# Adding a residual on VectorE out of PSUM, and normalising n3 on ScalarE, in a transformer block

## The reference, cut to what matters

```
h  = layernorm(x) * (1 + ca) + sa
y  = h + linear_attention(h)                  # 16 heads of 8
x1 = layernorm(y) * g1 + beta1
z  = x1 + relu(x1 @ W1 + b1) @ W2 + b2
x2 = x + ga * (layernorm(z) * g2 + beta2)
h2 = layernorm(x2) * (1 + cb) + sb
r, k = token-shift mixes of h2 with h2 of the token before, through W_r and W_k
out = x2 + gb * sigmoid(r) * (relu(k)^2 @ W_v)
```

## Time and profile before

| | |
|---|---|
| runs | 168.03, 169.07, 170.93 us; median 169.07 us |
| profiled execution | 167.34 us, of which the span is 165.5 us |
| busy, share of the span | PE 95%, PEld 88%, DVE 78%, ACT 72%, POOL 61% |
| granted TensorE clock | 0.998 of full speed |
| three stretches | fill (to 43.98 us), 11 equal steps (to 140.44 us), drain and tail (to 165.5 us) |

### The profile page before, as it was taken

The page is one execution under the profiler, slowest core; times in us unless marked ns, Lnnn a source line. Parts: engine busy times, 40 slices in busy tenths (PEclk is TensorE's granted clock), DMA queues, the critical chain, the costliest instruction groups (busy, mean ns, idle before and its releaser), DMA issues. The chain is left out here.

```text
span 165.5 us, 4067 instructions
## 1 busy us (share of the span) xinstructions
PE 157.5 (95%) x1161; PEld 146.1 (88%) x1161; DVE 129.5 (78%) x587; ACT 118.7 (72%) x323; POOL 101.2 (61%) x237
## 2 busy tenths in 40 slices
PE   7899799999999999999999999999999999999973
PEld 7767689889999999999999999999999999788862
DVE  3745757789797979798898978897979797987932
ACT  4365685969696969798796969696969694834562
POOL 4333366576576767767675757675757645476540
PEclk9999999999999999999999999999999999999999
DMA  4908929900010101000010101010101010100112
GB/s 130 315 21 256 307 87 295 417 19 0 0 34 4 32 0 34 2 26 10 0 36 2 32 6 32 0 32 4 34 2 34 2 32 0 36 0 4 32 36 63
DMA packets 8174, 9.95 MB, mean 60 GB/s; under 512 B 692, under 2 KB 6360, under 8 KB 8152
## 3 DMA queue, kind: packets, MB, share of 16 engines
q1 hardware_dynamic: 7712, 9.41, 17.8%
q10 hardware_dynamic: 440, 0.28, 0.6%
HBM read 7.55 MB, written 2.13 MB: 59 GB/s over the span
## 5 line engine op out<-in xcount | busy, mean ns | idle before, releaser
L986 PE MATMUL bank<-w,hid 128*128 128x128 f32 x240 | 31.5, 275 | 0.0
L1018 PE MATMUL bank<-x1T,w 128*128 128x256 f32 x120 | 30.9, 380 | 0.0
L986 PEld LDWEIGHTS bank<-w,hid 128*128 128x128 f32 x240 | 29.3, 192 | 0.0
L296 ACT ACTIVATE hT<-bank,modT 128x256 f32<-128x256 f32 x16 | 9.0, 565 | 21.5 <-PE bank L975 21.4
L1018 PEld LDWEIGHTS bank<-x1T,w 128*128 128x128 f32 x120 | 21.5, 190 | 2.5 <-ACT x1T L300 0.2
L461 POOL TENSOR_TENSOR rstd_n<-vare_n,power 128x2 f32<-128x2 f32 x30 | 21.3, 711 | 2.3
L457 POOL TENSOR_TENSOR vare_n<-mv_n,eps 128x2 f32<-128x2 f32 x30 | 5.9, 197 | 20.8 <-DVE mv_n L577 20.8
L274 ACT ACTIVATE n<-x_all,shift_n,rstd_n 128x128 f32<-128x128 f32 x32 | 13.9, 485 | 2.5 <-POOL shift_n L469 2.5
L583 DVE TENSOR_SCALAR ny<-bank,mv_ny,rstd_ny 128x128 f32<-128x128 f32 x32 | 11.7, 406 | 4.1 <-POOL rstd_ny L461 3.7
L568 DVE BATCH_NORM_STATS2 stats_z<-bank 128x6 f32<-128x128 f32 x30 | 7.4, 288 | 8.7 <-PE bank L986 8.7
L457 POOL TENSOR_TENSOR vare_z<-mv_z,eps 128x2 f32<-128x2 f32 x14 | 2.8, 196 | 18.5 <-DVE mv_z L577 18.5
(11 more groups left out here) (187 smaller groups left out, 469.2 us busy)
## 6 DMA issues: line engine op xcount, KB each, us to landing
gm_rows<-mod_rows_dram SPq DMA_DIRECT2D x2, 960.0 KB, 8.8
out<-out_sb SPq DMA_DIRECT2D x15, 128.0 KB, 1.9
gm_rows<-mod_rows_dram SPq DMA_DIRECT2D x1, 768.0 KB, 6.0
w<-in_w SPq DMA_DIRECT2D x1, 512.0 KB, 5.6
bv_row<-bv_rows_dram SPq DMA_DIRECT2D x1, 512.0 KB, 10.0
x_all<-in_x SPq DMA_DIRECT2D x1, 384.0 KB, 4.6
bv_row<-bv_rows_dram SPq DMA_DIRECT2D x1, 384.0 KB, 3.6
gm_rows<-mod_rows_dram SPq DMA_DIRECT2D x1, 384.0 KB, 4.3
```

What stands on the lines that cost most here:

```text
L986: last = nc.tensor.matmul(banks[6][:, c * D:(c + 1) * D], hid[:, f, c * 128:(c + 1) * 128], w2[:, f, :], start=False, stop=(f == FF - 1 an ...
L1018: return nc.tensor.matmul(bank[:, f % 2 * L:(f % 2 + 1) * L], w1[:, f * 128:(f + 1) * 128], x1T[:, :], start=True, stop=True)
```

## The change

- x1 is now written by rows. `scaled_y` reads y out of bank 1 and writes (y - mean) * g1 into `y_g1`, before 1/sqrt of the variance is there; `write_x1` multiplies by that and adds the row beta1 + b2. The result is in `ny`, of which there are two buffers now. The rows g1, beta1 and b2 come by a new DMA of 192 KB into `const_rows`, the last on ACT's queue at the start; one DVE instruction in step 0 adds beta1 and b2, after a wait for it.
- PE transposes that ny; ACT now copies it into x1T. PE no longer turns x1T back: 2 transposes less for each sequence, and the first product of z starts bank 6 itself.
- `add_x1` on DVE adds ny to bank 6 and writes `zx` in SBUF. The statistics of z and `centred` read zx. PE may write bank 6 again once zx is written (zx_ok), not after `centred` (z1_ok).
- n3 leaves DVE: POOL makes its shift in two small instructions (`shift_of_n3`), after the scale of ny, and ACT writes n3 (`take_n3`) as the last thing of a step, in the drain too, where x1T of the last sequence comes behind it.
- In the tail zx is made for each half of sequence 15.

```diff
+            act.dma_start(const_rows[:, :, :], a["rows"].unsqueeze(0).broadcast_to([128, 3, D])).then_inc(crows_loaded, 16)
...
+            def take_n3(s):
+                need(act, h2T_mm, s)
+                act.wait_ge(shift_ok, s + 1)
+                for c in range(NC):
+                    last = nc.scalar.activation(n3[:, c, :], x2[s % 3][:, c, :], ACT.Identity, scale=rstd["n3"][:, c:c + 1],
+                                                bias=shift_n3[:, c:c + 1])
+                last.then_inc(n3_ok, 1)
...
-                    nc.scalar.activation(x1T[:, :], banks[7][:, 0:L], ACT.Identity, scale=cols[:, G1:G1 + 1],
-                                         bias=beta1_b2[:, :]).then_inc(x1T_ok, 1)
+                    nc.scalar.activation(x1T[:, :], banks[7][:, 0:L], ACT.Copy).then_inc(x1T_ok, 1)
...
+            def shift_of_n3(s):
+                need(pool, rstd_ok["n3"], s + 1)
+                nc.gpsimd.tensor_tensor(mean_n3[:, :], mv["n3"][:, :, 0], rstd["n3"][:, :], ALU.mult).then_inc(mean_n3_ok, 1)
+                need(pool, mean_n3_ok, s + 1)
+                need(pool, n3_ok, s)
+                nc.gpsimd.tensor_tensor(shift_n3[:, :], zero_pair[:, :], mean_n3[:, :], ALU.subtract).then_inc(shift_ok, 1)
...
+            def scaled_y(s):
+                y = chunked(banks[1])
+                need(dve, mv_ok["ny"], s + 1)
+                for c in range(NC):
+                    last = nc.vector.scalar_tensor_tensor(y_g1[:, c, :], y[:, c, :], mv["ny"][:, c, 0:1], g1_row,
+                                                          ALU.subtract, ALU.mult)
+                last.then_inc(yg_ok, 1)
+
+            def write_x1(s):
+                dve.wait_ge(yg_ok, s + 2)
+                need(dve, zx_ok, s - 1)
+                need(dve, rstd_ok["ny"], s + 1)
+                for c in range(NC):
+                    last = nc.vector.scalar_tensor_tensor(ny[s % 2][:, c, :], y_g1[:, c, :], rstd["ny"][:, c:c + 1], shift_row,
+                                                          ALU.mult, ALU.add)
+                last.then_inc(ny_ok, 1)
+
+            def add_x1(s):
+                need(dve, z_mm, s + 1)
+                nc.vector.tensor_tensor(zx[:, :, :], chunked(banks[6]), ny[s % 2][:, :, :], ALU.add).then_inc(zx_ok, 1)
+                need(dve, zx_ok, s + 1)
...
             def centred(s):
-                z = chunked(banks[6])
+                z = zx
...
-                    for c in range(NC):
-                        residual_into(banks[6], x1T, c)
```

More of the change, by code:

```diff
@@ L100, in build @@
         attT = sb("attT", [128, L])
-        ny = sb("ny", [128, NC, D])
+        ny = [sb(f"ny_{p}", [128, NC, D]) for p in range(2)]
+        y_g1 = sb("y_g1", [128, NC, D])
+        zx = sb("zx", [128, NC, D])
+        const_rows = sb("const_rows", [128, 3, D])
+        g1_row, shift_row = const_rows[:, 0, :], const_rows[:, 1, :]
         x1T = sb("x1T", [128, L])
@@ L354, in step @@
                     take_n1(t + 1)
+                if live(t - 3):
+                    take_n3(sp_)
                 if t == 1:
@@ L390, in _ @@
             hidden_of_last(3)
-            act.wait_ge(shift_ok, 1)
-            for c in range(NC):
-                last = nc.scalar.activation(n3[:, c, :], x2[s14 % 3][:, c, :], ACT.Identity, scale=rstd["n3"][:, c:c + 1],
-                                            bias=shift_n3[:, c:c + 1])
-            last.then_inc(n3_ok, 1)
+            take_n3(s14)
             act.wait_ge(kk_mm, s13 + 1)
@@ L799, in step @@
                     norm_mv("ny", sb_ + 1)
+                    scaled_y(sb_)
                 if y_first:
-                    normalise("ny", ny, lambda c: y[:, c, :], sb_ + 1, ny_ok)
+                    scaled_y(sb_)
+                    write_x1(sb_)
                 if t == S:
                     gated(sc)
-                if live(t - 3):
-                    take_n3(t)
                 if live(t):
                     if t == 0:
+                        dve.wait_ge(crows_loaded, 16)
+                        nc.vector.tensor_tensor(shift_row, const_rows[:, 1, :], const_rows[:, 2, :], ALU.add).then_inc(yg_ok, 1)
                         dve.wait_ge(const_pool, 9)
@@ L986, in feed_forward_out @@
                         last = nc.tensor.matmul(banks[6][:, c * D:(c + 1) * D], hid[:, f, c * 128:(c + 1) * 128], w2[:, f, :],
-                                                start=False, stop=(f == FF - 1 and c == NC - 1))
+                                                start=(f == 0 and c == 0), stop=(f == FF - 1 and c == NC - 1))
                 return last
@@ L1160, in _ @@
             hidden_of_last(3).then_inc(w1b_mm, 1)
-            pe.wait_ge(z1_ok, LAST)
+            pe.wait_ge(zx_ok, LAST)
             for c in range(NC):
                 dest = banks[(6, 1)[c]][:, c * D:(c + 1) * D]
-                nc.tensor.matmul(dest, x1T[:, tokens(c)], ident[:, :], start=True, stop=False, is_transpose=True)
                 for f in range(FF):
@@ L1167, in _ @@
                         pe.wait_ge(hid_last, f + 1)
-                    last = nc.tensor.matmul(dest, hid[:, f, tokens(c)], w2[:, f, :], start=False, stop=(f == FF - 1))
+                    last = nc.tensor.matmul(dest, hid[:, f, tokens(c)], w2[:, f, :], start=(f == 0), stop=(f == FF - 1))
                 last.then_inc(z_last[c], 1)
@@ L1268 @@
         "bk": attn["bk"],
+        "rows": np.stack([attn[n] for n in ("g1", "beta1", "b2")]),
         "bv": attn["bv"],
```

50 lines of the change are left out of this document (25 added, 25 removed).

## The result

The changed kernel takes 174.86 us (174.80 to 174.91, 4 runs) against 169.05 (168.03 to 170.93) for the kernel before, run on the same chip: a ratio of 1.036 [1.032, 1.041]. It is slower; 171.0 us was predicted, with 173.8 as the upper end. Runs of most kernels here, of the one before too, lie at two levels 1.5 to 2.1 us apart, and the traces at full clock show the difference before the first transposes of step 2 (at 18.1 to 18.5 us, or at 20.1 to 20.2); rows and spans are compared within one level, and for the change that is 173.1 - 165.5 = 7.6 us of span.

A forecast was written before the change was run, and what follows sets the result against it. PE was taken as the bound, busy throughout the 11 full steps of 8.77 us. Steps +1.4, fill 0 and tail +0.9 gave +2.3 us on the profiled 167.34, 169.6, put at 171.0 us for scattered runs; range 167.3 to 173.8.

The forecast's parts named there:

- The sum: Whole kernel: 11 steps +1.4, fill 0, tail +0.9, together +2.3 us on the profiled 167.34.
- PE saves 0.22 a step: PE, full step: two transposes fewer save 0.22 us, so a step without new waits lasts 8.55 us.
- add_x1, 0.40 + 0.04: DVE, head of the step: add_x1 takes 0.40 us plus 0.04 wait on its own result, delaying all behind by 0.44.
- So 0.10 more: DVE, centred: two SBUF inputs make the pair 0.10 us longer, ends 0 and, by contention, 0.40.
- rival 1: DVE, centred: out of SBUF not slower and not meeting out_sb; step 8.65 to 8.70, 168.5 us; chance 0.24.
- I take 0.20, as in the tail: DVE, centred beside POOL's out_sb: contention costs 0.20 us, making att 0.35 late.
- rival 2: DVE: out_sb stretches both centred instructions 0.19 each, wv_plus stretches write_x1; att 0.53 late, step 9.08, 173.7 us; chance 0.22.
- Of the two the larger counts: PE's new waits for att (0.35 late) and n3 (ready at 9.5) don't add; nearly the larger counts, step 8.90 us.
- ACT's pair fits: ACT, end of step: its n3 pair of 0.87 us fits into 1.55 us of idle time.
- the list of what would show the mechanism wrong: After-profile signs: the mechanism is wrong if DVE is never idle or if PE waits for ny.
- Start, 0: Start and fill: new load and first steps' savings sum to 0, between -0.5 and +0.3 us.
- Tail, +0.9: Drain and tail: later DVE chain, x1T behind n3 and one more half-width add_x1 cost +0.9 us, between 0 and +1.6.

The follow-up runs named there:

- e14: e11 with DVE's statistics of x for n1 moved, from step 4 on, to its idle time ahead of write_x1: 166.11 us, ratio 0.993.
- e11: e8 with zx kept in SBUF and out_sb moved behind the next step's gate weights, as in e2: 168.26 us, ratio 1.001.
- e12: e11 with att ahead of centred on DVE: 171.82 us.
- e13: Changed kernel with shift_n of n3 on DVE behind kvs, wv_plus one step later, xb behind write_x1: 174.23 us.
- e2: Changed kernel with POOL's out_sb moved behind the next step's gate weights, no longer beside centred: 170.63 us, ratio 1.020.
- e5: Changed kernel with add_x1 writing its sum back into PSUM bank 6, where statistics and centred read it: 171.37 us, ratio 1.020.
- e4: Kernel before with only n3 moved to ACT and its shift to POOL: 169.76 us, ratio 1.014.
- e9: Changed kernel with the last x1T taken ahead of sequence 13's n3 on ACT in the tail: 174.58 us.
- e6: e2 with POOL making the shift of n3 ahead of the scale of ny: 178.28 us, ratio 1.063.
- e10: e6 with POOL's wv_plus one step later and xb held until write_x1 has ended: 171.89 us.
- e1_att_first: Changed kernel with att ahead of centred on DVE in all full steps: 176.08 us, ratio 1.049; run again 175.94 us.
- e8: e5 with e10's wv_plus and xb edits, e9's tail order, and shift_n of n3 on DVE behind kvs: 167.97 us, ratio 1.000.

## Why the prediction was wrong, step by step

The sum was +2.3 on the span, +7.6 came. Of the 5.3 missed, 4.2 are in the steps (3.2 in nine of them, 9.25 to 9.31 for 8.90, and 0.9 in the one of 9.83), 0.4 in the start, 0.7 in the tail.

- **PE saves 0.22 a step: right.** e14 shows 8.55 with no wait.
- **add_x1, 0.40 + 0.04: right**, 0.46. Without contention att is then 0.07 late and costs 0.12 (e11), for the 0.15 of the prediction.
- **"So 0.10 more" for centred: wrong.** Alone, the pair out of SBUF lasts 0.52 and holds DVE 0.43 (e11), against 0.51 and 0.42 from PSUM. The 0.61 of x had another reason, which these runs don't give. So rival 1 was right on the pair itself; but it cannot be cheaper either, as the Trainium skill, VectorE: DVE Perf Modes, TRN2 errata, would have it: the two are equal here.
- **"I take 0.20, as in the tail": the failed step.** Contention costs 0.48 (0.91 less 0.43). What the 0.20 was a price of, the rows show one instruction at a time. In the tail before, the second instruction of x began 0.40 before the end of the second wv_gate (151.29 and 151.68) and ended 0.15 after it: 0.54 in place of 0.34, the 0.20. Here the second instruction of centred began 0.67 before the end of out_sb and ended 0.15 after it too: 0.82 in place of 0.34. The time lost is what is left of POOL's instruction, and out_sb at 2.64 to 3.37 stood in my own working. One row gave the sign and I took its size for the price. The row of n in the tail before (1.35 for 0.60, above) already had the full one, though for an instruction of another form. att was therefore 0.54 late and not 0.35, the figure of rival 2 (0.53), whose mechanism it is and to which I gave 0.22; only that it had 0.19 on each instruction, and all 0.48 are on the second.
- **mixT was not on my list.** I read the reserve of att, ny and n3. mixT starts at 92.10 in the kernel before and PE's product of it at 93.02; with the 0.62 found above its reserve was 0.30. It costs 0.11 a step in the changed kernel, 0.10 in e11, 0.32 and more in e12, where att is first. With 0.05 for att's transposes this makes rival 2's step of 9.08 into 9.25.
- **"Of the two the larger counts": right.** e13 takes away the wait for n3 and changes nothing. n3 came at 9.91, not at 9.5: POOL's scale of n3 took 0.90 for 0.69 and the small shift_n 0.30 for 0.20. Had att been in time, n3 would have cost about 0.27, as e2 and e5 show (8.84, 8.83).
- **ACT's pair fits: right** (e4, step unchanged). DVE was not the bound, as predicted.
- **ny: not among the forecast's waits.** In one step PE waited for it, 0.70 late, when write_x1 began behind wv_plus. This was on the list of what would show the mechanism wrong; it is worth 0.6 of the 7.6 us, and it is the write_x1 of rival 2.
- **Start, 0: wrong by 0.4.** The new load cost nothing (step 2 begins at 18.21 for 18.25); the first n3 did, in step 4: 36.24 for 35.64 on PE, with 0.35 of waiting for it. From the first u product of step 3 to that of step 4 it is 8.62 against 8.08, and again 8.08 in e13.
- **Tail, +0.9: +1.6 came.** Up to the last u product 0.28 is lost, at n3's transposes; from there on, ny's transposes lose 0.55 (centred began at 149.72, with wv_gate at 149.74 to 150.19, and took 0.88), x1T 0.69 more, the reserve gives 0.54 back as reckoned, and then each half of the last z pays an add in DVE's chain, 0.33 and 0.32. I counted one of these. e9 shows that x1T's order is worth only 0.3. DVE and ACT in the tail of the changed kernel, for the earlier trace rows:

```profile
149.72 0.88 DVE L717 SCALAR_TENSOR_TENSOR z<-zx,mv_z,gm_rows 128x128 f32<-128x128 f32 x2
...
153.54 0.61 DVE L622 SCALAR_TENSOR_TENSOR ny<-y_g,rstd_ny,const_rows 128x128 f32<-128x128 f32 x2
```
and ACT:

```profile
154.80 0.88 ACT L294 ACTIVATE n<-x,shift_n,rstd_n 128x128 f32<-128x128 f32 x2 [2.35 <-POOL shift_n L487]
155.58 0.36 ACT L385 ACTIVATE x1T<-bank 128x256 f32<-128x256 f32 x1
```

Where the expected gain of 2.4 us went is then settled: e11, with centred and write_x1 undisturbed, is no faster than before, because add_x1 makes DVE's chain from z to att and mixT 0.46 us longer, more than the reserves of 0.45 and 0.30. e11 spans 6.6 us less than the changed kernel. Of these, 4.2 to 4.4 go with the contention of centred alone (e2; e5, its later start of 1.9 us taken off). The rest is the late n3, write_x1 in the one step, and the tail, not taken apart further. Open is what sets the two levels of the start, what delays write_x1 in one step, and why some pairs of DVE last 0.61 and others 0.51.

## What to carry to other kernels

Work moved onto an engine that is only 86% busy is not free if it stands at the head of a chain that the bound engine waits for: list every tile of that chain that the bound engine takes, each with its reserve, and look first for independent work in the chain that can go into the engine's idle time; here one such pair was worth 7.2 us. If an edit gives a vector instruction a second SBUF input, look at what GpSimd runs at that moment, after all shifts have been added, and take each instruction by itself: the one that begins second is held, so its price is what is left of the other, not the figure of some other overlap. Here write_x1, 0.35 us later than usual and so second, lasted twice as long. Of two waits of one engine in a loop the larger counts, so mending the smaller shows nothing, and a mended one may be hidden by another that the mending itself has made.

## What the runs showed of the hardware

- A DVE pair of 128x128 with two SBUF inputs lasts 0.99 in place of 0.52 us beside a 128x256 addition on GpSimd (e2, the changed kernel); write_x1 lasts 1.16 in place of 0.61 when it begins behind wv_plus (e6, e10).
- Such an instruction is held until the GpSimd one has ended. In the kept traces, that of e1_att_first left out, 224 single instructions of this kind (z, x, ny) began with at least 0.22 us left of an out_sb, xb, wv_gate or wv_plus; all 224 ended 0.145 to 0.154 us after it. The GpSimd instruction that was there first keeps its time (out_sb 0.73 both, wv_plus 0.46).
- It works the other way too, where the DVE instruction begins first: in the ordinary steps of the changed kernel write_x1 lasts 0.61, and shift_n of n3 takes 0.30 for 0.20 and wv_plus 0.56 for 0.46. GpSimd's 128x2 power takes 0.90 to 0.91 us in place of 0.69 where DVE's qT, with both inputs in SBUF, began 0.05 to 0.06 before it (the changed kernel, e6, e8, e12), and 0.69 to 0.70 where qT began 0.03 to 0.05 after it (e2, e5, which have both cases in turn); in e13 one took 0.98 where qT began 0.02 after it. That was read from the traces, not tested by itself.
- A tensor_scalar with one input, out of SBUF into SBUF, is held as well: in the tail before, each n of 128x128 ended 0.08 us after xb or xb_last (0.66 and 0.76 in place of 0.34).
- A pair read from PSUM and one read from SBUF last the same when undisturbed, 0.51 and 0.52.
